# Two-layer MoE FFN, one core: expert weights split during layer 0, routed start moved up, both transpositions of a slot tile side by side

## What is computed

```python
x = x + L0_ffn(L0_cond(x, itok0))        # cond: per sequence a 64x64 matrix chosen by an index
x = x + L1_ffn(L1_cond(x, itok1, bias))

# L0_ffn: dense 512 -> 2048 -> 512, gelu, with top-2 of 8 rank-8 LoRA adapters
# L1_ffn: top-2 of 8 experts (hidden 352) and one shared expert (hidden 704):
logits = x @ gate_w; scores = softmax(logits); topk_w, topk_idx = top_k(scores, 2)
g = silu(einsum('td,edh->teh', x, w_gate)) * einsum('td,edh->teh', x, w_up)
routed = einsum('teh,ehd,te->td', g, w_down, comb)
shared = silu(x @ sw_gate) * (x @ sw_up) @ sw_down
out = routed + shared
```

## Time and profile before

| | us |
|---|---|
| timed runs | 1051.5, 1054.9 and 2602.5, median 1054.9 |
| profiled execution | 1050.1 |
| its span, first to last instruction | 1048.2 |
| TensorE busy | 1010.6 (96%) |
| VectorE, GpSimd, ScalarE busy | 524.3, 354.5, 314.4 |
| DMA | 136.4 MB, mean 130 GB/s |

### The profile page before, as it was taken

One profiled execution on the slowest core, in us unless ns is written; L12 is line 12 of the kernel. 1 busy time (PEld: TensorE's weight loads), 2 busy tenths in 40 slices (PEclk: granted clock), 3 DMA queues, 4 the chain that ended last, 5 costly groups with the idle time before them and its releaser, 6 DMA issues.

```text
span 1048.2 us, 14852 instructions
## 1 busy us (share of the span) xinstructions
PE 1010.6 (96%) x4893; PEld 837.2 (80%) x4895; DVE 524.3 (50%) x886; ACT 314.4 (30%) x550; POOL 354.5 (34%) x351
## 2 busy tenths in 40 slices
PE   8899999999999999999999999999989999999993
PEld 5678887888888887888867777778778999999992
DVE  3788777455565455555566333665543314443000
ACT  3743332211121112111242010301144545454541
POOL 4123245410000000000042000022168889898873
PEclk9999999999999999999999999999999999999997
DMA  7387543443433434453444101005155665665433
GB/s 239 130 297 272 161 136 122 166 161 114 140 123 121 153 128 161 142 181 123 138 159 151 41 1 41 1 1 198 58 187 108 163 163 142 141 146 119 80 61 40
DMA packets 51322, 136.41 MB, mean 130 GB/s; under 512 B 8708, under 2 KB 10004, under 8 KB 50772
## 3 DMA queue, kind: packets, MB, share of 16 engines
q1 hardware_dynamic: 36660, 108.15, 30.1%
q0 software_dynamic: 12432, 25.71, 12.4%
q10 hardware_dynamic: 2192, 2.08, 0.7%
HBM read 96.85 MB, written 39.07 MB: 130 GB/s over the span
## 4 chain that ended last, share of the span: by engine, by line
PE 85%; DVE 4%; POOL 4%; DMA 2%; issue 1%; ACT 1%; ACTq 1%; PEldq 0%; POOLq 0%; PEld 0%; DVEq 0%
PE ps_y L1687 6%; PE ps_y L1689 6%; PE ps_y L1688 5%; PE ps_h L1645 5%; PE ps_h L1647 5%; PE ps_h L1646 5%; PE ps_u L1700 3%; PE ps_u L1699 3%; PE ps_h L1933 2%; PE ps_y L1933 2%; PE ps_y L1928 2%; PE ps_y L1929 2%; PE ps_y L1856 2%; PE ps_y L1857 2%; PE ps_h L1840 2%; PE ps_h L1841 2%
## 5 line engine op out<-in xcount | busy, mean ns | idle before, releaser
L1202 DVE TENSOR_TENSOR h<-h,wb 128x512 f32<-128x512 f32 x64 | 44.4, 693 | 162.6 <-ACT h L903 162.5
L897 ACT ACTIVATE h<-ps_h,bias 128x512 f32<-128x512 f32 x64 | 44.0, 689 | 235.1 <-PE ps_h L1654 235.1
L685 POOL DMA_DIRECT2D s_raw<-in_sgu x8 | 4.3, 544 | 299.9 <-DVE g_lo L1210 192.1
L1687 PE MATMUL ps_y<-w_hi,g_hi 128*128 (+1 forms) x256 | 102.2, 399 | 3.5 <-DVE g_lo L1210 3.5
L1689 PE MATMUL ps_y<-w_hi,g_lo 128*128 (+1 forms) x256 | 101.2, 395 | 0.0
L1688 PE MATMUL ps_y<-w_lo,g_hi 128*128 (+1 forms) x256 | 101.0, 395 | 0.0
L1645 PE MATMUL ps_h<-xt_hi,w_hl 128*128 128x512 f32 x256 | 100.0, 391 | 0.7 <-ACT lg_t L846 0.7
L1647 PE MATMUL ps_h<-xt_hi,w_hl 128*128 128x512 f32 x256 | 100.3, 392 | 0.0
L1646 PE MATMUL ps_h<-xt_lo,w_hl 128*128 128x512 f32 x256 | 100.2, 391 | 0.0
L1477 DVE CAST eg_hi<-e_raw 128x704 fp32r<-128x704 f32 x32 | 16.7, 581 | 138.0 <-PE ps_y L1958 125.3
L903 ACT ACTIVATE h<-ps_h,bias 128x512 f32<-128x512 f32 x64 | 43.9, 688 | 115.4 <-PE ps_h L1667 115.4
(11 more groups left out here) (319 smaller groups left out, 2455.5 us busy)
## 6 DMA issues: line engine op xcount, KB each, us to landing
w_hl<-w1s_d SPq DMA_DIRECT2D x49, 704.0 KB, 4.1
w1s_d<-w_hl SPq DMA_DIRECT2D x16, 704.0 KB, 5.9
e_raw<-in_wgu SPq DMA_DIRECT2D x8, 1408.0 KB, 7.1
w_raw<-in_w1b SPq DMA_DIRECT2D x16, 608.0 KB, 4.7
xres<-in_x SPq DMA_DIRECT2D x16, 256.0 KB, 4.5
acc<-x_d SPq DMA_DIRECT2D x4, 1024.0 KB, 7.6
xc_d<-xc SPq DMA_DIRECT2D x4, 1024.0 KB, 4.8
e_raw<-in_wdn SPq DMA_DIRECT2D x8, 512.0 KB, 8.4
```

Source lines behind the costliest of these rows:

```text
L1202: tt(h1[u][:], h1[u][:], wb[:, v, :], ALU.mult).then_inc(gch, 1)
L1687: mm(ps_y[:, j, :], g_hi[u][:, cols], sl(w2_hi), start=first, **kw)
```

## The change

1. **Experts 1 to 7 are split during layer 0.** The host lays their weights out as we1 (7, 128, 6 x 768), which is 42 units of 128 x 768 (384 KB). One unit goes with each step from 16 to 57: GpSimd loads it, ScalarE casts it after the step's second gelu, VectorE subtracts in place after `hidden_tile`, and GpSimd stores both halves in e_d. Layer 1 loads the halves straight into eg_hi, ed_hi, eg_lo and ed_lo (`load_halves`, 4352 KB in four DMAs); the loads of experts 2 to 7 wait, on SyncE now, until the buffer is free. Expert 0 is still loaded raw and split by VectorE.
2. **The bias column of cond1** is a 65th column of the matrix; its DMAs are gone, and `load_matrix` is called within GpSimd's loop over w1.
3. **Routed arithmetic.** x_low, products and g_low move from GpSimd to VectorE and read PSUM; the copies xg_f, ru and rgt_f are gone; xg_hi and xg_lo have two buffers. On GpSimd, iteration t is gather(t+5), scatter_add(t).
4. **Start and order.** gather(0) and gather(1) stand before the wait for the last gate/up; turn_x(0) stands after the last super-tile's first down product, turn_x(1) between gate and up of tile 0; in `slot_tile` turn_x(t+2) stands behind turn_g(t), ahead of up.

```diff
@@ SyncE
-            for s in range(NS):
+            def load_halves(e):
+                b, gu = e % 2, DC * 2 * H1
+                for k, (eg, ed) in enumerate(((eg_hi, ed_hi), (eg_lo, ed_lo))):
+                    sp.dma_start(eg[:, b].rearrange("p c n -> p (c n)").bitcast(F32),
+                                 e_d[e - 1, k, :, 0:gu]).then_inc(half_in, 16)
+                    sp.dma_start(ed[:, b].rearrange("p c n -> p (c n)").bitcast(F32),
+                                 e_d[e - 1, k, :, gu:gu + HC * D]).then_inc(half_in, 16)
+
+            for s in range(NS - 1):
                 store_acc(s)
+            for u in range(2):
+                sp.wait_ge(pre_st[u], 32 * (AHEAD // 2))
+            sp.wait_ge(gu_done, NS * SH)
+            load_halves(1)
+            store_acc(NS - 1)
             for e in range(1, E):
-                load_expert(e)
+                if e >= 2:
+                    tiles = sp.value_load(last_tile[0:1, e:e + 1], min_val=0, max_val=SLOT_TILES)
+                    sp.wait_ge(ry_done, 1 + tiles)
+                    load_halves(e)
+                sp.wait_ge(half_in, 64 * e)
+                sp.wait_ge(e_done, e)
+                sp.sem_inc(e_done, 1)
@@ GpSimd
             for f in range(FT):
                 low_w1(f, f % 2)
-            with pool.Fori(0, J) as j:
                 for h in range(2):
-                    load_matrix(pool, cw1, 1, SEQ, cw1_in[h], j, h)
+                    load_matrix(pool, f, h)
+
+            pool.wait_ge(w1_lo_done, 2 + FT)
+            pool.wait_ge(w2_lo_done, FT)
+            pool.wait_ge(z_ok, 4)
+
+            def load_unit(k):
+                u = k % 2
+                if k >= 2:
+                    pool.wait_ge(pre_st[u], 32 * (k // 2))
+                at = k % UNITS * UW
+                pool.dma_start(pre_raw[u], we1[k // UNITS, :, at:at + UW]).then_inc(pre_in[u], 16)
+
+            def store_unit(k):
+                u = k % 2
+                pool.wait_ge(pre_lo_done, k + 1)
+                at = k % UNITS * UW
+                for n, src in enumerate((pre_hi[u].bitcast(F32), pre_raw[u])):
+                    pool.dma_start(e_d[k // UNITS, n, :, at:at + UW], src).then_inc(pre_st[u], 16)
+
+            load_unit(0)
+            load_unit(1)
+            for k in range(AHEAD):
+                store_unit(k)
+                if 1 <= k < AHEAD - 1:
+                    load_unit(k + 1)
...
-            pool.wait_ge(gu_done, NS * SH)
             gather(0)
             gather(1)
+            pool.wait_ge(gu_done, NS * SH)
             nc.gpsimd.memset(rg[:, H1:HC * P], 0.0).then_inc(rg_zero, 1)
-            x_low(0)
-            products(0)
-            x_low(1)
             pool.wait_ge(sy_done, NS * TPS)
             for t in range(2, 5):
                 gather(t)
             for t in range(SLOT_TILES):
-                g_low(t)
-                if t + 1 < SLOT_TILES:
-                    products(t + 1)
-                if t + 2 < SLOT_TILES:
-                    x_low(t + 2)
                 if t + 5 < SLOT_TILES:
                     gather(t + 5)
-                if t:
-                    scatter_add(t - 1)
-            scatter_add(SLOT_TILES - 1)
+                scatter_add(t)
@@ ScalarE
+            def high_unit(k):
+                act.wait_ge(pre_in[k % 2], 16 * (k // 2 + 1))
+                nc.scalar.copy(pre_hi[k % 2], pre_raw[k % 2]).then_inc(pre_hi_done, 1)
...
                     gelus(s * FT + f, f, f % 2, s - 1 if f == 1 else None)
+                    if (s - 1) * FT + f < AHEAD:
+                        high_unit((s - 1) * FT + f)
@@ VectorE
+            def low_unit(k, u):
+                dve.wait_ge(pre_hi_done, k + 1)
+                tt(pre_raw[u].bitcast(F32R), pre_raw[u], pre_hi[u].bitcast(F32), ALU.subtract).then_inc(pre_lo_done, 1)
...
                                 hidden_tile(m * 2 + (s * FT + u), v, u)
+                                if (s - 1) * FT + b * 2 <= AHEAD:
+                                    low_unit(m * 2 + ((s - 1) * FT + u), u)
...
+            def x_low(t, u):
+                dve.wait_ge(xg_hi_done, t + 1)
+                tt(xg_lo[u][:].rearrange("p c n -> p (c n)"), ps_u[:, 0, :],
+                   xg_hi[u][:].rearrange("p c n -> p (c n)").bitcast(F32), ALU.subtract).then_inc(xg_lo_done, 1)
...
+            def slot_tile(t, u, nxt=True, nxt2=True):
+                g_low(t)
+                if nxt2:
+                    x_low(t + 2, u)
+                if nxt:
+                    products(t + 1, 1 - u)
@@ TensorE
+                    if (s, j) == (NS - 1, 0):
+                        turn_x(0, 0, 16, first=True)
...
                 if nxt:
                     gate_or_up(t + 1, 1 - u, after, 0)
                 turn_g(t)
+                if nxt2:
+                    turn_x(t + 2, x_buf, n)
                 if nxt:
                     gate_or_up(t + 1, 1 - u, after, 1)
-                if nxt2:
-                    turn_x(t + 2, x_buf, n)
                 down_routed(t, u, this)
```

More of the change, by code:

```diff
@@ L21, with adaln_ffn @@
 LORA_SCALE = 2.0
-def adaln_ffn(nc, x, itok0, itok1, side, cond0, router0, router0_b, w1b, b1, b2, b2s,
-              cond1, gate1, wgu1, wdn1, sgu1, sdn1, out):
+def adaln_ffn(nc, x, itok0, itok1, cond0, router0, router0_b, w1b, b1, b2, b2s,
+              cond1, gate1, wgu1, wdn1, we1, sgu1, sdn1, out):
     N = x.shape[0]
@@ L96, in adaln_ffn @@
                              for u in range(2)])
+        ahead = ExitStack()
+        sb_ahead = tensors(ahead)
+        pre_hi = [sb_ahead(f"pre_hi{u}", [P, UW], F32R)[:] for u in range(2)]
+        pre_raw = [sb_ahead("pre_raw0", [P, UW])[:], u1t[:, 0:UW]]
+        ahead.close()
         w_raw = [sb(f"w_raw{u}", [P, WROW]) for u in range(2)]
@@ L339, in adaln_ffn @@
         out_st = sem("out_st")
+        pre_in = [sem(f"pre_in{u}") for u in range(2)]
+        pre_hi_done = sem("pre_hi_done")
+        pre_lo_done = sem("pre_lo_done")
+        pre_st = [sem(f"pre_st{u}") for u in range(2)]
+        half_in = sem("half_in")
         e_in = sem("e_in")
@@ L1231, in low_s @@
                     dve.wait_ge(z_done, 2 + STEPS)
+                else:
+                    for u in range(2):
+                        dve.wait_ge(pre_st[u], 32 * (AHEAD // 2))
                 hi, lo, raw = shared_halves(n)
@@ L1544, in _, with products, g_low @@
                             split_expert(0, 0, k)
[L1547 to L1553 removed]
+            def x_low(t, u):
+                dve.wait_ge(xg_hi_done, t + 1)
+                tt(xg_lo[u][:].rearrange("p c n -> p (c n)"), ps_u[:, 0, :],
+                   xg_hi[u][:].rearrange("p c n -> p (c n)").bitcast(F32), ALU.subtract).then_inc(xg_lo_done, 1)
+            def products(t, u, first=False):
+                dve.wait_ge(rs_done, t + 1)
+                dve.wait_ge(rup_done, t + 1)
+                if not first:
+                    dve.wait_ge(rgt_done, t)
+                tt(rg[:, 0:H1], rs[:], ps_y[:, u, 0:H1], ALU.mult).then_inc(rg_done, 1)
+            def g_low(t):
+                dve.wait_ge(rgt_hi_done, t + 1)
+                tt(rgt_lo[:].rearrange("p c n -> p (c n)"), ps_u[:, 1, 0:HC * P],
+                   rgt_hi[:].rearrange("p c n -> p (c n)").bitcast(F32), ALU.subtract).then_inc(rgt_lo_done, 1)
+            def slot_tile(t, u, nxt=True, nxt2=True):
[4 more added lines that the diff above has]
+                    products(t + 1, 1 - u)
+            x_low(0, 0)
+            x_low(1, 1)
+            products(0, 0, first=True)
+            for t in range(2):
+                slot_tile(t, t)
+            with dve.Fori(1, (SLOT_TILES - 2) // 2) as m:
+                for u in range(2):
+                    slot_tile(m * 2 + u, u)
+            for t in range((SLOT_TILES - 2) // 2 * 2, SLOT_TILES):
+                slot_tile(t, t % 2, t + 1 < SLOT_TILES, t + 2 < SLOT_TILES)
         @block.tensor
@@ L1869, in slot_sums, with turn_x @@
                 last.then_inc(oh_mm, 1)
+            def turn_x(t, u, n, first=False):
+                pe.wait_ge(xg_in[u], n)
+                if not first:
+                    pe.wait_ge(xg_lo_done, t)
+                for c in range(DC):
+                    last = nc.tensor.transpose(ps_u[:, 0, c * P:(c + 1) * P], xg[u][:, c * P:(c + 1) * P], ident[:])
+                last.then_inc(xgt_done, 1)
             cond_rows(2)
@@ L1906, in experts @@
                 return [(packed // E ** n % E, packed // E ** n % 2) for n in range(WINDOW)]
-            def turn_x(t, u, n, first=False):
-                pe.wait_ge(xg_in[u], n)
-                if not first:
-                    pe.wait_ge(xg_f_done, t)
-                for c in range(DC):
-                    last = nc.tensor.transpose(ps_u[:, 0, c * P:(c + 1) * P], xg[u][:, c * P:(c + 1) * P], ident[:])
-                last.then_inc(xgt_done, 1)
             def gate_or_up(t, u, eb, k):
@@ L1932, in gate_or_up @@
                 for c in range(DC):
```

(3 more changed lines are left out.)

118 lines of the change are left out of this document (41 added, 77 removed).

## The result

The changed kernel takes **1067.5 us** (median of 4 runs, 1063.8 to 1069.6). The kernel before, on the same chip, takes 1053.8 (median of 4, one of them 2602.5). The ratio is 1.0133, with a 95% interval of 1.0091 to 1.0176: a little slower, and less than the 2% that was named as what can be told. The profiled execution took 1069.6 us, with a span of 1067.9; that of before had 1048.2, so 19.7 us are to be explained.

The account below looks back on a forecast made before the run. TensorE, busy for 96% of the span, was taken as the bound. Layer 0's +32 us, routed gains of 6, 3, 3.5 and 4.6, and +1 of risk made +16 on 1050.1: 1066 us, range 1031 to 1108.

Parts of the forecast that it names:

- rival A: Layer 0: the units are hidden, X under 5.4 since stores don't hold up a load; 1034 us, chance 0.20.
- The closed loop on GpSimd: Layer 0, steps 16 to 57: load, cast, subtraction, stores, next load take 8.4 us against a 7.39 us step; 32 us delay.
- X: Layer 0: time from issue of a unit's first store to landing of the load behind it, 6.4 us (4.6 to 9.7).
- Rival B: Layer 0: the unit's load moves beside w_hl, so X is 7.2, the loop 9.2, the delay 64; 1098 us, chance 0.32.
- The two changes of super-tile are longer than three steps and are inside these times: Layer 0: the changes of super-tile get no charge of their own beyond the 32 us delay.
- The w_hl load: Layer 0: has 7.2 us of cover for a 4.1 us landing; a doubled landing puts one more us on TensorE's path.
- Start: Start of routed tiles: earlier gathers and transpositions remove TensorE's waits and the clock stays up; 6 us gained.
- Tiles: Routed tiles: 3.0 us gained as GpSimd's arithmetic leaves, 3.5 from putting both transpositions side by side.
- Tail: End of routed part: each scatter follows its own copy, so the last starts at 1034.9, not 1039.49; 4.6 us gained.
- rival D: Routed part: serial scatters become the bound under the doubled load, so routed gains don't come; 1078 us, chance 0.05.
- Late halves: Routed part: an expert's doubled load, 19.4 us, just fits its 20.5; 1 us charged, bounds 0 and 15.
- Rival C: Routed part: halves of three experts each come 5 us late, with scatters falling behind; 1080 us, chance 0.08.

Follow-up runs that it names:

- experiment 4: The changed kernel without the units' loads, casts, subtractions and stores in layer 0, expert halves loaded from the unsplit weights: 1034.9 us, ratio 0.9848.
- experiment 8: The changed kernel with a third store per unit, the low half once more, ahead of the next load: 1148.0 us, ratio 1.0911.
- Experiment 6: The changed kernel with one store per unit, the next load issued ahead of that store, and mask copies ahead of the cast: 1034.7 us, again 1033.5.
- experiment 11: The kernel of Experiment 6 with the start of the routed part (gathers and transpositions of tiles 0 and 1) as before: 1037.4 us against 1033.5.
- experiment 10: The kernel of Experiment 6 with the transposition for tile t+2 back behind the up product of tile t+1: 1035.3 us, ratio 0.985.
- experiment 9: The changed kernel without the loads of the low halves from expert 3 on: 1066.2 us, ratio 1.0151.
- experiment 2: The changed kernel with the load of unit k+1 issued ahead of the two stores of unit k: 1053.0 us, ratio 1.001.
- experiment 3: The changed kernel with the load of unit k+1 ahead of the stores of unit k and mask copies ahead of the cast: 1060.6 us, ratio 1.008.
- experiment 5: The changed kernel storing only each unit's low half, the high half loaded from the unsplit weights: 1057.8 us, ratio 1.0073.

## Why the prediction came out, and where it was wrong

The prediction had 1066 and the time is 1067.5. The sum is right in its routed half, where experiment 4 has 1034.9 without the units and the prediction's rival A 1034, though its terms for the tail and within the tiles err. In layer 0 the 32 us came out by luck: its mechanism there, an even loss in every step, would have given 0 to 8 us with the measured loop, and the 34 us arose where it had put nothing.

- **The closed loop on GpSimd** was the right thing to look at. Its links, the cast at 0.83 and the subtraction at 0.96 are as worked out, and experiment 8 lengthens it (casts 10.4 us apart). Experiment 6 opens it: there the loads are early and 14 us of ScalarE's waiting are left.
- **X was mis-sized**: 6.4 was taken from four loads of 352 KB; it measured 5.4 to 5.5, on the edge of rival A (5.4). Stores land faster than the loads they were likened to: the two stores 2.6 and 3.8 us after their issue, the load behind them 4.3. So the loop is 7.6 us, not 8.4, and the even loss of 0.9 us per step isn't there. With X = 5.45 the working gives 7.47 for the loop and 40 x 0.08 = 3 us of delay; with the measured 7.59 it gives 8. Its own absolute times give nothing at all: the cast of unit 2 would end at 183.3 + 5.45 + 0.85 = 189.6, that of unit 41 at 189.6 + 39 x 7.59 = 485.6, ahead of 486.7. (By them the delay ends at X of some 5.6, not 5.4, since the steps at the changes count as time in which the loop catches up.)
- **Rival B** said that the unit's load would be held up by w_hl, issued some 2 us behind the first store. It is issued 2.0 to 4.0 us behind it, and X stays at 5.3 to 5.9 in the even passes, so B did not come. With a third store it did (experiment 8).
- **Bursts**: the even traffic of the rows stood for all steps. Where SyncE's queue moves xres, acc and x besides, X is 7.7 to 9.6; these places cost some 11 of the 34 us (4.4 at steps 18 to 20, 6.6 at 54 to 56).
- **"The two changes of super-tile are longer than three steps and are inside these times"** is the step that failed, and on the other side. Two steps there come 3.3 us apart, VectorE has its sums in front of the subtraction, and the loop is 12.2 us just there: 10.7 + 7.0 us. Both are in the timelines of before (its VectorE ends the last operation of step 32 at 300.23, 5.2 us after the second gelu), had I followed unit 16 through VectorE's order as I did unit 1.
- **The clock after a stop** was charged at the start of the routed tiles (1.8 us) and left out in layer 0, where it makes at least 7 of the 34 us.
- **The w_hl load** was said to cost one more us if its landing doubled. It did, once: at step 60, beside four loads of s_raw that stood behind the last units, 2.2 us.
- **Start** (6): the distance from the first gate product to the first output copy went from 16.7 to 11.6, and the wait of 0.91 ahead of it is gone: 6.0. Of this the moved fill is 1.8 (experiment 11), so the term was right as a sum, and the larger part is left for the arithmetic that left GpSimd. A wait of 2.2 us among the shared down products, which both kernels have, gave 1.5 us back in this profile, since the clock fell behind it (last section): hence the +0.6 in the table.
- **Tiles** (3.0 + 3.5): from first to last output copy 258.3 became 251.2, so 7.2 in place of 6.5. The side-by-side transpositions are 1.8 of it (experiment 10), half their term (0.1 x 38 is 3.8, and the sum has 3.5); the rest, 5.4, is left for the arithmetic and the splits that are gone, which no run tried alone. Two errors that cancel.
- **Tail** (4.6): it is 2.7, give or take the 1.3 by which two profiles of one kernel differ. The last scatters:

```profile
1048.13 1.55 POOL L801 DMA_INDIRECT out_x<-yt,slot_tok  x1 [4.00 <-DMA out_x<-yt,slot_tok]
1053.51 1.55 POOL L801 DMA_INDIRECT out_x<-yt,slot_tok  x1 [3.83 <-DMA out_x<-yt,slot_tok]
1059.28 1.55 POOL L801 DMA_INDIRECT out_x<-yt,slot_tok  x1 [4.22 <-DMA out_x<-yt,slot_tok]
```

  The copy of tile 37 starts at 1050.88, and its scatter could start at 1051.6; it starts at 1053.51, since a backlog stands ahead of it. The term forgot it. The backlog builds up beside the loads of the experts' halves:

```profile
831.28 1.58 POOL L801 DMA_INDIRECT out_x<-yt,slot_tok  x1 [3.97 <-ACT yt L1046]
...
841.14 1.59 POOL L801 DMA_INDIRECT out_x<-yt,slot_tok  x1 [6.99 <-DMA out_x<-yt,slot_tok]
```

  9.9 us from one scatter to the next, where 5.6 is normal; five more such places follow, of up to 11.6 us. The four output buffers take it: TensorE's tiles keep their 6.7 us, so rival D did not come. What spoke for D, ScalarE waiting for scatters before, is the same misreading as in experiment 9: it is idle for 1.2 us before nearly every output copy there, whatever the view names.
- **Late halves** (1, up to 15): TensorE never waits for one. Rival C did not come.
- **The rule of the Trainium skill**, page "DMA: Bandwidth & Descriptors", section on the anatomy of one SWDGE DMA, gives by estimate 4.7 us for the 1.18 MB of the three DMAs. The trace has about 5.4 with traffic beside it, so that estimate was 0.7 us short, the four loads 1.0 us long. What the prediction concluded from it, nothing lost, nearly held for the normal steps alone.

## What to carry to other kernels

Background work that closes a loop (load, compute, store, next load) must be checked at the shortest step and the busiest place of every engine in the loop, not at the mean step; a loop that is 0.2 us longer than the step costs little, and one irregular step costs 10 us. Reordering the issues moves such a loop, fewer bytes shorten it a little, and here neither alone hid it, but both together (with the masks first) did. And behind an in-order engine it is the operation after the waiting one that counts: moving one victim out of the way only names the next.

## What the runs showed of the hardware

- A stop of TensorE costs more than its length. In experiment 2 it stands still for 4.13 us, and the stretch behind has (244 to 249 us, then 249 to 252):

```profile
244.00:249.00 5.00, 0.87 (x3) 0.45 (x2) 1.06 (x2) 1.42 (x2) 0.00 (x0) 0.92 0.74 270
249.00:252.00 3.00, 3.00 (x9) 2.31 (x9) 2.87 (x5) 0.69 (x1) 1.60 (x3) 0.57 0.47 78
```

  A granted clock of 0.57 is near its lower level, 1.2 of 2.4 GHz. The delay of this stop is 5.8 us, 4.1 of waiting and 1.6 of slow matmuls. Waits of 0.9 us (experiment 11) leave the clock at 1.00. The Trainium skill, page "TensorE: Matmul & The Clock Gate", section "Wait — 56ns, not 53.3ns?", has 426.7 ns from one start to the next for 512 columns on the lower clock; the 0.43 us of the trace agree.
- The length of a stop doesn't settle whether the clock falls. All kernels have a wait of 2.1 to 2.2 us among the last shared down products. Behind it the granted clock fell in 5 of the 13 profiles taken with the change or a variant of it, and where it fell the way from the last gelu of layer 0 to the first routed gate product is 1.5 us longer (232.3 against 230.8). The changed kernel, where it fell, and experiment 3, where it didn't:

```profile
728.00:733.00 5.00, 4.81 (x14) 3.80 (x15) 3.68 (x4) 0.00 (x0) 4.05 (x2) 0.66 0.00 0
...
721.00:726.00 5.00, 4.65 (x20) 3.84 (x21) 3.84 (x4) 0.00 (x0) 3.89 (x2) 1.00 0.00 0
```

- TensorE took the full-width weight as its high operand in place of the rounded one (experiment 5), at the same pace (251.2 us from first to last output copy, as with the rounded one); a stored high half isn't needed for the routed products of this kernel.
- A scatter that adds takes 5.6 us from one to the next on this queue, and 9.9 to 11.6 us while expert halves load, with 280 to 340 GB/s on the DMA engines; halving those loads shortens the slow one by about 1 us (9.2 to 10.0).
